# A layernorm, gated recurrence and block-quantised FFN on one core: 1 / std by Ln, Exp and a Newton step, six gamma kv terms on VectorE, and a run of transposes ahead of the first work

## What is computed

```python
def _layernorm(x, eps=1e-05):
    return (x - mean(x)) / sqrt(var(x) + eps)

xn = _layernorm(x)                       # (16, 512, 128)
# gated recurrence along the 512 rows
r, k, v = split(xn @ W_rkv + b_rkv)
r = sigmoid(r);  k = exp(k);  kv = k * v
lam = exp(-exp(nu_log));  gamma = exp(nu_log + gamma_log) - 1
u1 = scan(lam, kv);  u2 = scan(lam, k)   # y_t = lam * y_{t-1} + x_t
s = ((u1 + gamma * kv) / (u2 + gamma * k + 1e-6) * r) @ W_o + b_o
# FFN with inputs and weights rounded to a grid in blocks of 32
g = silu(dequantised(xn) @ dequantised(W_ffn).T + b_ffn)
out = x + s * g
```

## Time and profile before

| | us |
|---|---|
| median of 3 runs | 125.94 (125.5 to 125.95) |
| the profiled execution | 125.42 |
| its span, from the first to the last instruction | 123.6 |

### The profile page before, as it was taken

How to read it: one execution, slowest core, us unless ns; L and a number is a source line. 1 busy time by engine, 2 the same in 40 slices (tenths; PEclk the granted TensorE clock), 3 DMA queues, 4 the chain that set the end, 5 groups by cost and what they waited for, 6 DMA issues and landing times.

```text
span 123.6 us, 1670 instructions
## 1 busy us (share of the span) xinstructions
PE 109.6 (89%) x387; PEld 58.5 (47%) x387; DVE 105.1 (85%) x167; ACT 104.7 (85%) x180; POOL 106.4 (86%) x127
## 2 busy tenths in 40 slices
PE   0008989999999999999999999999999999999980
PEld 0006444444555555555455555544654655554450
DVE  0446999999998999999999948998969989993881
ACT  4047799999999999999969899999999979999800
POOL 2288699999997999999999999999999999998400
PEclk9999999999999999999999999999999999999999
DMA  2879930000020000110201020200102002012026
GB/s 66 248 237 402 386 127 0 0 3 0 0 90 5 0 0 26 59 58 27 85 0 65 25 85 0 85 0 3 72 15 90 0 3 85 31 54 85 0 85 255
DMA packets 6025, 8.82 MB, mean 71 GB/s; under 512 B 1536, under 2 KB 1920, under 8 KB 6016
## 3 DMA queue, kind: packets, MB, share of 16 engines
q1 hardware_dynamic: 5040, 8.72, 19.4%
q10 hardware_dynamic: 976, 0.00, 0.4%
HBM read 4.53 MB, written 4.19 MB: 71 GB/s over the span
## 4 chain that ended last, share of the span: by engine, by line
POOL 39%; ACT 17%; PE 16%; issue 12%; DVE 9%; DMA 3%; ACTq 1%; DVEq 1%; POOLq 0%
POOL den L302 8%; POOL mixed L308 7%; PE taken_ps L946 6%; POOL rstd L256 6%; POOL q L279 6%; ACT L679 4%; POOL xd L286 4%; PE v_ps L968 4%; POOL gk L296 3%; ACT den L744 3%; DMA x_all<-in_L_attn_inputs_dram 3%; PE turned_ps L925 3%; POOL xn L271 2%; ACT gate L739 2%; DVE kv L451 2%
## 5 line engine op out<-in xcount | busy, mean ns | idle before, releaser
L946 PE MATMUL taken_ps<-xnT,wrkv_sb 128*128 128x512 f32 x64 | 33.0, 611 | 0.3 <-ACT recept L731 0.3
L696 ACT ACTIVATE xn<-x_all,shift,rstd 128x128 f32<-128x128 f32 x48 | 19.8, 486 | 6.4 <-POOL shift L260 6.4
L308 POOL TENSOR_TENSOR mixed<-mixed,den 128x512 f32<-128x512 f32 x16 | 20.3, 1277 | 1.8 <-DVE mixed L478 1.7
L679 ACT ACT_TABLE_LOAD x16 | 20.5, 1283 | 1.0 <-PEq L1170 0.7
L302 POOL TENSOR_TENSOR den<-den,gk 128x512 f32<-128x512 f32 x16 | 20.4, 1279 | 1.0 <-DVE den L460 0.8
L469 DVE TENSOR_TENSOR_SCAN num_ps<-own_ps,kv 128x512 f32<-128x512 f32 x16 | 19.5, 1217 | 0.2
L460 DVE TENSOR_TENSOR_SCAN den<-own_ps,k 128x512 f32<-128x512 f32 x16 | 19.2, 1204 | 0.3 <-POOL mixed L308 0.3
L925 PE MATMUL turned_ps<-ident,xn 128*128 128x128 f32 x64 | 10.4, 292 | 9.6 <-POOL xn L271 9.6
L422 DVE BATCH_NORM_STATS2 stats<-x_all 128x6 f32<-128x256 f32 x32 | 11.8, 415 | 7.3 <-DMA x_all<-in_L_attn_inputs_dram 7.3
L279 POOL TENSOR_TENSOR q<-xn,inv_scale 128x512 fp8e4<-128x512 f32 x16 | 16.8, 1053 | 1.1 <-DVE inv_scale L443 1.1
L968 PE MATMUL v_ps<-xnT,wrkv_sb 128*128 128x512 f32 x32 | 17.2, 619 | 0.0
(11 more groups left out here) (62 smaller groups left out, 181.0 us busy)
## 6 DMA issues: line engine op xcount, KB each, us to landing
x_all<-in_L_attn_inputs_dram SPq DMA_DIRECT2D x16, 256.0 KB, 6.6
out_dram<-x_all SPq DMA_DIRECT2D x16, 256.0 KB, 2.0
wrkv_sb<-in_L_attn_W_rkv_dram SPq DMA_DIRECT2D x1, 192.0 KB, 4.4
wf_sb<-in_L_ffn_weight_dram SPq DMA_DIRECT2D x1, 64.0 KB, 6.4
wo_sb<-in_L_attn_W_o_dram SPq DMA_DIRECT2D x1, 64.0 KB, 6.1
cols<-in_L_attn_nu_log_dram ACTq DMA_DIRECT2D x1, 0.5 KB, 3.9
cols<-in_L_attn_gamma_log_dram ACTq DMA_DIRECT2D x1, 0.5 KB, 4.2
cols<-in_L_attn_b_o_dram ACTq DMA_DIRECT2D x1, 0.5 KB, 4.6
```

What stands on the lines that cost most here:

```text
L308: nc.gpsimd.tensor_tensor(mixed[:, n % MIX, :], mixed[:, n % MIX, :], den[:, n % DEN, :], ALU.mult)\
L679: act.add_instruction(mybir.InstLoadActFuncSet(name=nc.get_next_instruction_name(), engine=mybir.EngineType.Activation, act_func_set_id=n, ...
L696: ins = nc.scalar.activation(xn[:, n % XN, j * D:(j + 1) * D], x_all[:, n, j * D:(j + 1) * D], ACT.Identity, bias=shift[:, t:t + 1], scale ...
L946: nc.tensor.matmul(taken_ps[i % 2][:, :], weights, moving, start=True, stop=True).then_inc(filled, 1)
```

## The change

1. **1 / std.** For the three batches of four sequences (3, 4 and 5) GpSimd's power is gone. `deviations(b)` (the first two operations of the old `inv_std`) is a step of its own, ScalarE then makes a rough 1 / std by Ln and Exp (`rough_std(b)`), and `inv_std(b)` makes one Newton step from it with four small GpSimd operations. The batches 0, 1 and 2 keep the power.
2. **gamma kv.** For sequences 2, 5, 7, 9, 11 and 13 the addition of gamma * kv to `num_ps` is a `scalar_tensor_tensor` on VectorE; the other ten stay on TensorE.
3. **Run of transposes.** TensorE begins with 32 transposes of the identity into the bank `v_ps`, which nothing reads; they wait for the identity alone.
4. **Orders.** The lists of calls of all four engines, `TURNS` and `TAKEN` are new. The table sets are loaded 14 times.

The diff, cut to its core:

```diff
+    WARM_UP = 32
+    NEWTON_TILES = 16
+    NEWTON_FIRST = next(i for i, (lo, hi) in enumerate(STAT_BATCHES) if (hi - lo) * TPP >= NEWTON_TILES)
...
-            def inv_std(b):
+            def deviations(b):
...
+            def inv_std(b):
+                lo, hi = (tile(n, 0) for n in STAT_BATCHES[b])
+                if hi - lo < NEWTON_TILES:
+                    deviations(b)
+                    pool.wait_ge(var_ready, b + 1)
+                    nc.gpsimd.tensor_tensor(rstd[:, lo:hi], var[:, lo:hi], minus_half[:, 0:hi - lo], ALU.pow)\
+                        .then_inc(rstd_ready, 1)
+                else:
+                    i = b - NEWTON_FIRST
+                    pool.wait_ge(rough_ready, i + 1)
+                    nc.gpsimd.tensor_tensor(newton[:, lo:hi], var[:, lo:hi], rough[:, lo:hi], ALU.mult)\
+                        .then_inc(newton_step, 1)
+                    pool.wait_ge(newton_step, 3 * i + 1)
+                    nc.gpsimd.tensor_tensor(newton[:, lo:hi], newton[:, lo:hi], rough[:, lo:hi], ALU.mult)\
+                        .then_inc(newton_step, 1)
+                    pool.wait_ge(newton_step, 3 * i + 2)
+                    nc.gpsimd.tensor_scalar(newton[:, lo:hi], newton[:, lo:hi], -0.5, 1.5, ALU.mult, ALU.add)\
+                        .then_inc(newton_step, 1)
+                    pool.wait_ge(newton_step, 3 * i + 3)
+                    nc.gpsimd.tensor_tensor(rstd[:, lo:hi], rough[:, lo:hi], newton[:, lo:hi], ALU.mult)\
+                        .then_inc(rstd_ready, 1)
...
+            def gamma_kv(n):                      # on VectorE
+                dve.wait_ge(num_scanned, n + 1)
+                nc.vector.scalar_tensor_tensor(num_ps[:, :], kv[:, n % KS, :], gam[:, 0:1], num_ps[:, :],
+                                               ALU.mult, ALU.add).then_inc(num_done, 1)
...
+            def rough_std(b):                     # on ScalarE
+                lo, hi = (tile(n, 0) for n in STAT_BATCHES[b])
+                i = b - NEWTON_FIRST
+                act.wait_ge(var_ready, b + 1)
+                nc.scalar.activation(log_var[:, lo:hi], var[:, lo:hi], ACT.Ln).then_inc(log_var_ready, 1)
+                act.wait_ge(log_var_ready, i + 1)
+                nc.scalar.activation(rough[:, lo:hi], log_var[:, lo:hi], ACT.Exp, scale=-0.5).then_inc(rough_ready, 1)
...
+            def warm_up():                        # on TensorE
+                pe.wait_ge(ident_ready, 1)
+                for i in range(WARM_UP):
+                    nc.tensor.transpose(v_ps[:, 0:P], ident[:, :], ident[:, :])
```

More of the change, by code:

```diff
@@ L84, in build @@
         rstd = sb("rstd", [P, SEQS * TPP])
+        log_var = sb("log_var", [P, SEQS * TPP])
+        rough = sb("rough", [P, SEQS * TPP])
+        newton = sb("newton", [P, SEQS * TPP])
         shift = sb("shift", [P, SEQS * TPP])
@@ L587, in _ @@
             scan_num(5)
-            residual(1)
+            gating(2)
+            gamma_kv(5)
+            scan_den(4)
+            residual(2)
+            receive(5)
             key_values(6)
+            scan_den(5)
             statistics(13)
-            scan_den(4)
-            gating(2)
+            scan_num(6)
+            key_values(7)
+            scan_den(6)
             block_maxima(5)
-            scan_den(5)
-            residual(2)
-            scan_den(6)
-            receive(5)
@@ L598, in _ @@
             statistics(14)
+            statistics(15)
+            key_values(8)
             gating(3)
-            key_values(7)
-            scan_num(6)
-            residual(3)
-            key_values(8)
             block_scales(5)
             inverse_scales(5)
-            statistics(15)
             receive(6)
+            key_values(9)
+            scan_num(7)
+            residual(3)
+            gamma_kv(7)
+            key_values(10)
+            receive(7)
+            gating(4)
+            scan_num(8)
@@ L649, in _ @@
-            scan_den(12)
-            scan_den(13)
             gating(9)
@@ L668, in _ @@
             gating(13)
+            residual(12)
             gating(14)
-            residual(12)
             gating(15)
@@ L778, in _ @@
             normalise(2)
+            rough_std(3)
+            keys(1)
             normalise(3)
-            keys(1)
             silu_phase()
@@ L801, in _ @@
+            exp_phase()
+            logarithm(0)
+            keys(2)
+            copy_wdT()
+            copy_xnT(4)
+            inverse(0)
+            logarithm(1)
+            keys(3)
+            normalise(6)
+            copy_xdT(1)
+            keys(4)
+            inverse(1)
+            copy_xnT(5)
+            silu_phase()
+            gates(0)
             gates(1)
-            normalise(6)
+            copy_xnT(6)
+            copy_xdT(2)
+            normalise(7)
             receptance(4)
-            copy_xnT(5)
@@ L836, in _ @@
+            inverse(3)
+            normalise(10)
+            copy_xdT(5)
             logarithm(4)
+            copy_xnT(10)
             keys(8)
+            logarithm(5)
+            keys(9)
             inverse(4)
-            logarithm(5)
+            logarithm(6)
+            keys(10)
+            rough_std(5)
             inverse(5)
-            keys(9)
-            copy_xnT(10)
-            copy_xdT(5)
-            logarithm(6)
+            inverse(6)
+            silu_phase()
+            gates(4)
@@ L1080, in _ @@
+            values(8)
+            transpose_xn(10)
+            project(3)
+            gamma_kv(6)
+            transpose_xd(6)
+            keys(10)
+            values(9)
+            transpose_xd(7)
+            ffn(4)
+            untranspose(3)
+            values(10)
+            ffn(5)
+            project(4)
+            receptance(8)
             receptance(9)
             untranspose(4)
-            transpose_xd(7)
-            ffn(5)
-            gamma_kv(7)
+            transpose_xn(11)
@@ L1085, in _ @@
+            ffn(6)
+            receptance(10)
+            gamma_kv(8)
+            transpose_xn(12)
             project(5)
-            values(10)
-            transpose_xn(11)
-            receptance(10)
-            ffn(6)
+            ffn(7)
+            transpose_xd(8)
+            receptance(11)
+            values(11)
             untranspose(5)
-            keys(10)
-            transpose_xn(12)
+            keys(11)
+            transpose_xn(13)
+            keys(12)
+            transpose_xd(9)
@@ L1113, in _ @@
             keys(13)
             transpose_xd(10)
+            gamma_kv(10)
+            untranspose(6)
+            ffn(8)
+            values(12)
+            project(7)
+            ffn(9)
+            receptance(12)
+            untranspose(7)
+            receptance(13)
+            transpose_xn(14)
             project(8)
-            gamma_kv(11)
+            values(13)
             transpose_xn(15)
+            transpose_xd(11)
             untranspose(8)
-            values(13)
             keys(14)
-            receptance(13)
+            keys(15)
```

472 lines of the change are left out of this document (211 added, 261 removed), and 16 rows, old and new, of tables (TAKEN, TURNS).

## The result

The changed kernel takes 120.29 us (median of 4 runs, 120.27 to 120.87) against 125.72 for the kernel before on the same chip: a ratio of 0.9586, interval 0.9539 to 0.9634. The profiled execution took 120.27, its span is 118.5. The forecast was 125.1, with 123.7 to 127.3 as range: the time lies 3.4 us under the lower end, and the span under what the prediction called VectorE's floor, 119.1. Executions over 1.5% above the fastest of the same kernel are left out of the ratios.

What follows compares the result with a forecast made beforehand. It took TensorE to set the pace, the others close behind. Afterwards VectorE's floor of 119.1 plus 3.7 idle gave a span of 122.8; adding 2.34 gave 125.1 us, range 123.7 to 127.3.

Steps and rivals of the forecast that it cites:

- VectorE's floor: VectorE's start at 10.32, its work of 106.2 and 2.59 us of store: the span's floor, 119.1 us.
- Part 4, the orders: New call lists cost the waits they cause; ScalarE reaches the last batch at 65.0, span no lower than 121.6.
- small gaps: VectorE's short idle times in the 90 us to 110: 1.0 us in all.
- real waits: VectorE's waits for other engines in the middle of the kernel: 0.5 us, most earlier ones gone.
- Part 1: Six gamma kv moved: TensorE loses 5.2 us, VectorE gains 4.1, bounds 3.6 to 4.8.
- TensorE sets the pace: From 31.38 to 116.43 TensorE's queue is 99% full by starts, 84.2 of 85.05 us, others close behind.
- The rival that TensorE was no bound: VectorE's second-half waits stay and 4.1 us of work come on top: time up to 130, chance 0.05.
- Part 2: In three large batches a Newton step replaces GpSimd's power: GpSimd saves 5.0 us, ScalarE net 1.4 less.
- The gain is slack: GpSimd's and ScalarE's savings on 1 / std set no end; they only let VectorE's waits go.
- The rival of the late handover: GpSimd waits at the last batch's 1 / std for ScalarE: time 126.5 to 128.5, chance 0.18.
- Part 3: 32 early transposes delay nothing, speed TensorE's first transposes and keys by some 1 us each; gain 0 to 0.4.
- What would show it: Signs of being right: TensorE gaps mid-kernel, VectorE 98 to 99% full, operation 0.74, batches 1.3 to 1.7, transposes 0.11.

Runs made afterwards that it cites:

- e14_after_narrow: Kernel after with VectorE's gamma kv of the six sequences over 32 of 512 columns: 119.96 to 121.96 us, ratio 0.9588.
- e11, e15, e16, e5, e8, e12: A follow-up kernel with the 32 transposes ahead; the text given does not say which change it made or its time.
- e1: Kernel after with gamma kv of the six sequences back on TensorE: 126.58 us, ratio 1.0074.
- e2: Kernel after with the power back on GpSimd in the three large batches: 126.16 us in one execution, 128.35 to 129.45 in three.
- e18: Kernel after with the power back on GpSimd in the three large batches, measured once more: 129.43 us, ratio 1.0290.

## Why the prediction was wrong

Span forecast 122.8, measured 118.5, 4.3 less, by the prediction's own terms (behind 10.32):

| | forecast | measured |
|---|---|---|
| VectorE's work | 106.2 | 103.25 |
| idle from 10.32 to its end | 3.7 | 2.33 |
| from there to the end | 2.59 | 2.6 |

Of the 4.3 us, 3.0 are in the first row and 1.4 in the second. Two steps of the prediction failed.

**Part 4, the orders: the step that failed first.** It took them as a source of waits ("they cost what they make engines wait"), looked for one late place, and put there a chain that allowed nothing below 121.6. Its length came out and its beginning didn't. ScalarE was to reach the rough 1 / std of batch 5 at t = 65.0: 53.9 us of its work, and 11.1 idle as before. These rows of after show ScalarE at the last batch, and GpSimd's last ratio:

```profile
60.57 0.22 ACT L805 ACTIVATE log_var<-var 128x16 f32<-128x16 f32 x1
```

```profile
110.75 1.28 POOL L341 TENSOR_TENSOR mixed<-mixed,den 128x512 f32<-128x512 f32 x1 [0.51 <-DVE mixed L520]
```

It is there at 60.57, 4.4 earlier, after 52.4 us of work and 8.2 idle, of which 0.2 lie after 20 us (in before, 2.64 between 20 and 70). From there to the end of the last ratio at 112.03 are 51.5 us, the forecast's figure, in part by luck, since the wait for the last receive in it is 0.51 and not 1.69; and from there to the end of the span 6.5 (6.7 forecast). So the waits that ScalarE had in before were carried into lists in which it has none. With the parts alone it keeps waiting (2.30 us at 66.09 in the old lists). The runs show that this is where the gain is: with the parts in both, the new lists are 7.5 us faster than the old ones, and without the parts they gain nothing. For VectorE it appears as idle time: 0.40 from 20 us to the last 12, against the 1.5 forecast for small gaps and real waits, and 1.49 at the end against 1.8. The rate of 0.90 in 50 us, called "small gaps of a full engine", was mostly avoidable: after shows 0.27 in the same stretch.

**VectorE's floor: no floor.** This is the larger term of the sum. VectorE's busy time was carried over as a constant, 102.12 and 4.1 more. Of the 2.95 us that it came out too high, 0.84 moved ahead of 10.32 into the waits for loads (3.83 us of work there, 2.99 before). Some 0.9 is operations that take another time in another place: five small ones 0.45 less together (wd 291 ns for 1020, wscale 314 for 620, wos_sb 209 for 443, against gam_diag 599 for 366 and wq 879 for 294), and the many others, gatings and scans first, some 0.45. Some 1.1 is overlap: operations that don't wait overlap the one before, by about 0.06 each. The durations of all VectorE operations add up to 115.7 us before and 119.1 in after, 3.4 more, but the busy time grew by 2.0 only.

**Part 1: right in the price, half right in what bounds.** 730 ns measured, 0.74 forecast. Undoing it in the new lists costs 5.3 to 6.1, for a forecast 5.2 of TensorE's queue. But "TensorE sets the pace" was half true: its queue was full by starts, and in the old lists taking 4.2 us from it gave 0.4, and moving the six gamma kv to VectorE cost 0.7. Full is not the same as alone in leading. The rival that TensorE was no bound fell as to the time (130), but in the old lists it comes near: there a matmul taken off bought nearly nothing, as the prediction had it follow from the rule that it cites from the Trainium skill (Perfetto Trace Analysis, Identifying the Most-Contended Engine). In the new lists it did buy its size. The weight loads' share itself went from 47 to 52% and doesn't tell these two states apart.

**Part 2: right, but for what its gain is worth.** The batch's four steps and the shift take from 15.55 to 17.00, 1.45 (1.3 to 1.7 forecast); the wait for the statistics was 0.74, not 1.7, because VectorE takes them earlier in its new list. GpSimd -5.8 (forecast -5.0), ScalarE -2.7 (-1.4). "The gain is slack" holds in the old lists. In the new ones it is a condition: without it 126.2 to 130.2. The rival of the late handover did not come about; no GpSimd operation of batch 5 waits for the rough value.

**Part 3: mis-sized.** 0 to 0.4 forecast, some 1.0 measured by taking it out of the new lists, and a loss of 0.8 in the old ones. Its reason was wrong too: the first transposes still go at half pace (8 from 9.45 to 11.14, 0.21 each, 0.11 forecast). What the run does instead stays open.

**What would show it**, as listed: VectorE 99.5% full, yes; the operation and the batches, yes; real gaps of TensorE in the middle, no. Its starts stand 0.86 and 0.44 apart from 26 us on, as before: four engines became nearly full at once.

**What stays open.** Which places of the new lists carry the gain was not taken apart; only all of them were exchanged. The chain that ended last lies to 73% on TensorE in after, 16% before: whether TensorE alone leads in after is not settled, since relief was tried there on VectorE only. Against it stands that 4.1 us added to VectorE cost 3.7. No version was clearly faster than the kernel after.

## What to carry to other kernels

Where several engines are some 95% full or more and their orders are fixed, expect little from a relief by itself (0 to 15% of its size here) and price an addition at most of its size (60 to 90%); here the gain needed the relief and lists laid out anew for it, and neither alone showed it. When a chain is laid through such lists, don't carry the waits of before into its beginning. A floor made of an engine's busy time moves with the order, by work that slips into early waits, by overlap, and by operations that take another time in another place; here by 3 us in 106. Undo each half of such a change before crediting one.

## What the runs showed of the hardware

In TensorE's first work the clock looked as if it followed the gap. In after, 1.91 us without work stand ahead of 9.45; with the longer run 0.53. The stretch from 9 to 12 of after, then that of the longer run:

```profile
9.00:12.00 3.00, 2.55 (x9) 0.61 1.05 404
```

```profile
9.00:12.00 3.00, 2.59 (x11) 1.00 1.05 404
```

Granted 0.61 against 1.00, and the first two keys take 2.91 against 1.95. But other profiles speak against the length of the gap as the reason. TensorE in e14_after_narrow, with the same 32 transposes ahead:

```profile
1.56 5.31 PE L1010 MATMUL v_ps<-ident 128*128 128x128 f32 x32 [1.56 <-POOL ident L255]
9.54 1.42 PE L983 MATMUL turned_ps<-ident,xn 128*128 128x128 f32 x8 [2.67 <-POOL xn L304]
10.95 1.95 PE L1004 MATMUL taken_ps<-xnT,wrkv_sb 128*128 128x512 f32 x4
```

A longer gap, 2.67 us, and full pace behind it; the same in e11, e15 and e16 (2.56 to 2.67). In e1, e2, e5, e8 and e12 the gap is 1.62 to 2.06 and the pace behind it is half. In the four the run of 32 itself took 5.2 to 5.4 us, in the five and in after 5.9 to 6.4; why is open. Later gaps are as mixed: behind the 2.00 us at 81.88 in e2 a matmul took 1.92, behind the 2.00 at 84.61 in e18 it took 1.02. And e14, with its early full pace and less work for VectorE, was no faster than after by its ratio. Before, the rows showed 1.00 while the durations were those of half pace: durations decide.

The other surprise is the one above: a 128x4 operation of VectorE that takes 0.17 us or 2.45, and when it is long ends with a GpSimd operation.
